# One transformer-like kernel: streamed expert weights, causal masks applied after the exponential, and logits and z taken at other places

## The chip, the cores and the metric

The kernel runs on one NeuronCore of a Trainium2 chip. TensorE multiplies matrices into PSUM, VectorE (DVE), ScalarE (ACT) and GpSimd (POOL) work on tiles, and SyncE (SP) issues most transfers. The metric is the device time of one launch in microseconds (us).

## What is computed

For each of 64 samples: an image of 224 x 224 x 3 becomes 196 patch tokens of width 192 (layer norm over a patch with its four shifted copies, then one product), 128 text tokens are appended, attention with 12 heads is added, and a soft mixture of 64 experts is added. T = 324 tokens, D = 192, hidden width F = 768.

```python
# attention, 12 heads of 16, with a sink column
att = jnp.einsum('bhqd,bhkd->bhqk', q, k) * scale
att = jnp.where(causal[None, None], att, -jnp.inf)
att = jnp.concatenate([sink_col, att], axis=-1)
att = jax.nn.softmax(att, axis=-1)[..., 1:]
y = jnp.einsum('bhqk,bhkd->bhqd', att, v)
# experts
logits = jnp.einsum('sd,btd->bst', sl, tok)
dispatch_w = jax.nn.softmax(logits, axis=-1)
combine_w = jax.nn.softmax(logits, axis=-2)
y = jnp.einsum('btd,bst->bsd', xn, dispatch_w)
y = jnp.einsum('sio,bsi->bso', fc1_weight, y) + fc1_bias
y = jax.nn.gelu(y, approximate=False)
y = jnp.einsum('sio,bsi->bso', fc2_weight, y) + fc2_bias
out = jnp.einsum('bsd,bst->btd', y, combine_w)
```

## The kernel before

There are four stages. A prologue folds the norms into the weights. Then a software pipeline runs over the samples: step `b` works on attention of sample `b`, the embedding of `b + 2`, the q/k/v preparation of `b + 1` and the expert routing of `b - 1`. Every engine has its program for a step written out by hand; the engines meet only through semaphores (`Signal`), and each engine runs its own list strictly in order. The third stage runs the 64 experts over the routed tokens of all samples, the fourth mixes the expert outputs back into the residuals and stores them.

One step on TensorE: a first loop over 12 heads computes `scores` (query by key, only to find each row's maximum, which DVE takes with `negmax`). Between heads stand parts of other work: `turn(z)` at head 3, the logits (slots by `zt`) at heads 7 and 8, the transposed maxima (`maxima`) at head 8, the transposed logits at head 10. A second loop over 12 heads computes `scores_t` (key by query, with the maximum already subtracted through extra rows of `qst`), ACT exponentiates into `prob`, and `values` multiplies `prob` by `vaug` in three groups of four heads. Each group has three products, k = 0, 1, 2, one for each key tile. `scores_t` of head h waits until the exponential of head h - 2 is done, because there are two pairs of PSUM banks. Groups 0 and 1 are multiplied inside the second loop, group 2 behind it, then come the projections (`project`), the head transposes, `proj` and the next step.

The mask: `causal` holds -1e30 above the diagonal; in both loops a small product with the identity adds it to the diagonal block of the scores. In `scores_t` that is three products a head (127, 128 and 69 columns).

DVE in a step: the maxima of the 12 heads, `lmax` and `dmax` of the routing softmax, `stat1`, `h_new` and its norm `mv1` for sample `b + 2`, `xhat`, the divided heads, the rotary products `by_cos` and `by_sin`, the residual `h1`, its norm `mv2`, and z. GpSimd: `rot`, `rest`, the chain from `alpha` to `beta_t` (the logits' scale), the split of the maxima (`mpart`), `part`, then `rstd1` and `rstd2` for sample `b + 2`. ACT: among others z squared, `zt`, the first maxima `mt`, the scaled logits `logit`, `dexp` (right ahead of the 12 exponentials), the exponentials, `comb` and `yraw`.

In the expert stage, a slot is one expert. SP keeps eight slots of weights in flight and refills two when a `down` product is done. For each slot TensorE multiplies with a 97 x 128 block of `w1` stationary and the 64 samples of `y_all` moving (12 products), ACT takes the gelu, and `down` multiplies `act_t` (stationary) by `w2` (moving, 192 columns). DVE adds biases that SP has loaded broadcast over the samples. In the last stage groups of four samples are loaded, multiplied (`cw` by `ow`), added by DVE and stored by ACT's queue.

## Time and profile before

| | us |
|---|---|
| median of 3 runs | 3379.23 (3373.21 to 3383.34) |
| the profiled execution | 3375.94 |
| its span, first to last instruction | 3374.2 |
| steps of samples, about 220 to 2850 | 40.96 each |
| experts | 2853 to 3220 |
| wait, then mixing and stores | 3220 to 3374 |

The profiled execution's own time is 1.7 us above its span. PE is TensorE's matmuls, PEld its weight loads, which overlap them; the end of a matmul is modelled, so the distance from one start to the next says more than a duration. An fp32 product stands as two records in the trace. A number in square brackets behind a row is idle time of that engine ahead of it, and what ended it.

### The profile page before, as it was taken

What the parts mean: (1) busy time and instruction counts of PE and PEld (TensorE: products, weight loads), DVE (VectorE), ACT (ScalarE), POOL (GpSimd) and SP (SyncE); (2) the same over time, 40 slices, a digit from 0 to 9 for tenths busy, and PEclk for the clock granted to TensorE, in tenths of its full rate; (3) what the DMA queues carried; (4) which work ended last, traced back from release to release, by engine and by line L of the source; (5) the groups of instructions that cost most, each with busy time, mean ns of one, the idle gap of its engine ahead of it and who ended that gap; (6) DMA issues with size and microseconds to landing.
All of it is one profiled execution on the core that took longest, in us unless ns stands there. A gap on an engine that the chain in (4) does not pass through costs nothing. (4 is left out here: it accounts for less than half of the span.)

```text
span 3374.2 us, 76729 instructions
## 1 busy us (share of the span) xinstructions
PE 2923.5 (87%) x27714; PEld 2267.1 (67%) x27714; DVE 1702.9 (50%) x5384; ACT 1625.0 (48%) x3266; POOL 1220.0 (36%) x2197
## 2 busy tenths in 40 slices
PE   3079999999999999999999999999999986999945
PEld 2057777777777777777777777777777765888832
DVE  2436666666656566556666666666565552000023
ACT  0045665566666666666666655666665653000000
POOL 2134444444444444444444444444444441000000
PEclk8589999999999999999999999999999997776778
DMA  4233333333333333333333333333333322988979
GB/s 107 48 79 86 90 91 92 87 93 88 88 88 88 89 87 88 86 86 86 86 86 90 92 92 91 88 88 87 88 89 88 86 58 57 231 226 227 233 199 292
DMA packets 445437, 364.24 MB, mean 108 GB/s; under 512 B 32526, under 2 KB 424091, under 8 KB 444828
## 3 DMA queue, kind: packets, MB, share of 16 engines
q1 hardware_dynamic: 420956, 342.23, 39.4%
q10 hardware_dynamic: 24128, 17.42, 1.6%
q8 instruction: 207, 3.39, 0.4%
q14 instruction: 146, 1.20, 0.1%
HBM read 199.61 MB, written 43.25 MB: 72 GB/s over the span
## 5 line engine op out<-in xcount | busy, mean ns | idle before, releaser
L959 DVE TENSOR_REDUCE negmax<-ps 128x1 f32<-128x325 f32 (+2 forms) x2304 | 665.1, 350 | 100.1 <-PE ps L605 92.3
L560 PE MATMUL ps<-window_w,xp 108*98 108x193 f32 x2304 | 507.4, 339 | 107.2 <-ACT xp L812 107.2
L812 ACT ACTIVATE prob<-ps 128x590 f32<-128x590 f32 x768 | 505.2, 662 | 185.1 <-PE ps L628 170.4
L603 PE MATMUL ps<-kst,qst 99*128 99x325 bf16 (+2 forms) x2304 | 394.5, 251 | 82.9 <-DVE negmax L959 82.9
L560 PEld LDWEIGHTS ps<-window_w,xp 108*98 108x98 f32 x2304 | 338.5, 167 | 110.6 <-ACT xp L812 107.3
L1147 POOL TENSOR_TENSOR rot<-by_cos,by_sin 96x324 f32<-96x324 f32 x128 | 111.8, 873 | 682.0 <-DVE by_sin L1043 681.9
L603 PEld LDWEIGHTS ps<-kst,qst 99*128 99x128 bf16 (+1 forms) x2304 | 224.0, 104 | 195.4 <-DVE negmax L959 116.5
L605 PE MATMUL ps<-causal,ident_b 128*128 128x128 bf16 (+1 forms) x2304 | 333.6, 213 | 0.0
L769 PE MATMUL ps<-xt,wqk 97*96 97x324 f32 (+1 forms) x1024 | 320.6, 446 | 1.7 <-ACT xt L812 1.7
L644 PE MATMUL ps<-prob,vaug 128*32 128x324 f32 (+2 forms) x4608 | 286.4, 341 | 0.1
L1277 PE MATMUL ps<-y_all,w 97*128 (+3 forms) x1536 | 233.8, 326 | 29.9 <-DMA w<-in_L_ffn_fc_weight_dram 29.0
L1277 PEld LDWEIGHTS ps<-y_all,w 97*128 97x128 f32 (+1 forms) x1536 | 227.1, 238 | 43.3 <-issue 34.2
L1030 DVE RECIPROCAL rden<-ps 98x12 f32<-98x12 f32 (+1 forms) x192 | 43.4, 226 | 381.3 <-PE ps L788 381.3
L622 PE MATMUL ps<-qst,kst 102*128 102x295 bf16 x768 | 228.6, 298 | 2.5 <-ACT prob L812 1.3
L812 ACT ACTIVATE xp<-xw 108x1764 f32<-108x1764 f32 x64 | 219.8, 3434 | 8.2 <-DMA xw<-in_x_dram 8.2
L605 PEld LDWEIGHTS ps<-causal,ident_b 128*128 128x128 bf16 (+1 forms) x2304 | 203.7, 103 | 14.7 <-issue 0.3
L769 PEld LDWEIGHTS ps<-xt,wqk 97*96 97x96 f32 (+1 forms) x1024 | 157.5, 165 | 83.2 <-issue 4.9
L1351 DVE TENSOR_TENSOR pair_out<-ps,biases 128x192 f32<-128x192 f32 x32 | 11.5, 358 | 359.1 <-PE ps L1264 311.5
L1318 ACT ACTIVATE act_t<-ps 128x384 f32<-128x384 f32 x64 | 31.4, 491 | 329.9 <-PE ps L1277 329.9
L625 PE MATMUL ps<-qst,kst 102*128 102x197 bf16 x768 | 189.8, 247 | 0.0
L1093 POOL TENSOR_TENSOR by_cos<-rot,part 96x648 f32<-96x648 f32 x128 | 185.4, 1468 | 0.0
L1127 POOL TENSOR_TENSOR part<-by_cos,part 96x648 bf16<-96x648 f32 x128 | 177.8, 1409 | 15.6 <-DMA qst<-part 12.9
(179 smaller groups left out, 6161.8 us busy)
## 6 DMA issues: line engine op xcount, KB each, us to landing
w<-in_L_ffn_fc_weight_dram SPq DMA_DIRECT2D x128, 576.0 KB
xw<-in_x_dram SPq DMA_DIRECT2D x384, 189.0 KB
qst<-part SPq DMA_DIRECT2D x768, 60.8 KB
kst<-part SPq DMA_DIRECT2D x768, 60.8 KB
h_held<-h_new SPq DMA_DIRECT2D x64, 288.0 KB, 4.3
residual_image<-h SPq DMA_DIRECT2D x64, 147.0 KB
h_i<-residual_image SPq DMA_DIRECT2D x16, 588.0 KB
out_dram<-h_i ACTq DMA_DIRECT2D x32, 294.0 KB
```

The costliest lines, as they stand in the source:

```text
L560: mm = pe.matmul(ps[0:TILE, BK7, half * (D + 1):(half + 1) * (D + 1)], xp[:, q, TILE * half:TILE * (half + 1)], window_w[:, q, :], start=( ...
L603: pe.matmul(ps[0:nq, bk, col:col + keys], qst[i][0:MAX_ROW, h, q0:q0 + nq], kst[i][0:MAX_ROW, h, 0:keys], start=True, stop=False)
L605: mm = pe.matmul(ps[0:nq, bk, col + q0 + 1:col + keys], ident_b[:, 0:nq], causal[:, 0:nq], start=False, stop=True)
L622: pe.matmul(ps[:, bank, 0:EXPC], k0, q[:, 0:EXPC], start=True, stop=False)
L625: pe.matmul(ps[:, bank + 1, c1:c2], k1, q[:, KTILES[1][2]:T], start=True, stop=False)
L644: mm = pe.matmul(ps[STRIP * s:STRIP * (s + 1), BK6, q0:T], vaug[i][0:nk, k, h, :], prob[0:nk, h % 8, col:col + T - q0], start=(k == 0), st ...
L769: mm = pe.matmul(ps[0:HALF, SC + 2 * side + e, 0:T], wqk[0:k, c, 2 * side + e, :], xt[0:k, c, 1:KEYS], start=(c == 0), stop=(c == 1))
L812: return nc.scalar.activation(out_, in_, f, **kw)
L959: last = dve.tensor_reduce(negmax[0:nq, q, h:h + 1], ps[0:nq, bk, col:col + q0 + nq + 1], AX.X, ALU.max, negate=True)
L1093: pool.tensor_tensor(rest[:, side], rot[:, side], part[0][:, side], ALU.subtract).then_inc(rest_ready.sem, 1)
L1127: pool.tensor_tensor(part[2][:, side], rest[:, side], part[1][:, side], ALU.subtract).then_inc(p3_ready.sem, 1)
L1277: mm = pe.matmul(ps[:, k % 4, B * f:B * (f + 1)], w1[k][0:kk, c, 128 * f:128 * (f + 1)], y_all[0:kk, c, one(s + k), :].rearrange("p o b -> ...
```

## The change

Attention. The three mask products of each head leave `scores_t`. Instead the diagonal blocks of the probabilities are set to zero after the exponential: for groups 0 and 1 by GpSimd (`affine_select`, three instructions a group, 4 x 127, 4 x 128 and 4 x 69 elements a partition), for group 2 by DVE (minimum with the tile `cap`, which is 1e30 or 0). `values` now waits for `capped` where it waited for the exponential. `prob` has 12 buffers in place of 8, groups 0 and 1 of `values` stand one head later, and the third product of group 1 behind the loop. ACT scales the logits ahead of the copy of the first maxima. DVE makes z behind the maxima of the next step's head 1, where it stood at the end of the step. The residuals and combine weights are stored in another layout, so that a group of four samples is one run for each partition.

Experts. Two slots go together. The samples of `y_all` are stationary and `w1` moves (384 columns at a time, the two slots in the two halves of the array's columns); the hidden layer is turned by six transposes (`turn`) and copied by DVE; the second bias is a product of its own. Weight rows are loaded as 6144 bytes of `w1` and 4608 bytes of `w2` for each partition in one run, where they were runs of 3072 and 768 bytes. All loops are written out.

```diff
-    himg = nc.dram_tensor("residual_image", (2 * B, TILE, D), F32, kind="Internal").ap()
-    htxt = nc.dram_tensor("residual_text", (B, TXT, D), F32, kind="Internal").ap()
-    cscr = nc.dram_tensor("combine_weights", (B, NS, T), F32, kind="Internal").ap()
+    himg = nc.dram_tensor("residual_image", (B // GROUP, TILE, GROUP, 2, D), F32, kind="Internal").ap()
+    htxt = nc.dram_tensor("residual_text", (B // GROUP, TXT, GROUP, D), F32, kind="Internal").ap()
+    cscr = nc.dram_tensor("combine_weights", (B // GROUP, 2, NS, GROUP // 2, T), F32, kind="Internal").ap()
...
+                        dve.wait_ge(cap_mm, 1)
+                        dve.tensor_scalar(cap[:], ps[:, 5, 0:128], -1.0, 1.0, ALU.max, ALU.add)
+                        dve.drain()
+                        dve.tensor_scalar(cap[:], cap[:], -MASKED, None, ALU.mult)
...
+                def cap_probs(engine, b, g):
+
+                    exp_ready.wait(engine, b, 4 * g + 4)
+                    h0, col = 4 * g, 0
+                    for k, (_, nk, q0) in enumerate(KTILES):
+                        first = 1 if k == 0 else 0
+                        nq = min(128, T - q0) - first
+                        p = prob[0:nk, h0:h0 + 4, col:col + nq]
+                        if g < 2:
+                            last = engine.affine_select(p, p, [[0, 4], [1, nq]], ALU.is_ge, 0.0, base=first,
+                                                        channel_multiplier=-1)
+                        else:
+                            allowed = cap[0:nk, first:first + nq].unsqueeze(1).broadcast_to((nk, 4, nq))
+                            last = engine.tensor_tensor(p, p, allowed, ALU.min)
+                        col += T - q0
+                    last.then_inc(capped.sem, 1)
...
-                        pe.matmul(ps[:, bank, 0:EXPC], k0, q[:, 0:EXPC], start=True, stop=False)
-                        pe.matmul(ps[:, bank, 0:127], causal[:], ident_b[:, 1:128], start=False, stop=True)
+                        pe.matmul(ps[:, bank, 0:EXPC], k0, q[:, 0:EXPC], start=True, stop=True)
                         pe.matmul(ps[:, bank + 1, 0:n0], k0, q[:, EXPC:T], start=True, stop=True)
-                        pe.matmul(ps[:, bank + 1, c1:c2], k1, q[:, KTILES[1][2]:T], start=True, stop=False)
-                        pe.matmul(ps[:, bank + 1, c1:c1 + 128], causal[:], ident_b[:], start=False, stop=True)
-                        pe.matmul(ps[:, bank + 1, c2:EXPC], k2, q[:, KTILES[2][2]:T], start=True, stop=False)
-                        pe.matmul(ps[:, bank + 1, c2:EXPC], causal[:], ident_b[:, 0:EXPC - c2], start=False,
-                                  stop=True).then_inc(st_mm.sem, 1)
+                        pe.matmul(ps[:, bank + 1, c1:c2], k1, q[:, KTILES[1][2]:T], start=True, stop=True)
+                        pe.matmul(ps[:, bank + 1, c2:EXPC], k2, q[:, KTILES[2][2]:T], start=True, stop=True
+                                  ).then_inc(st_mm.sem, 1)
...
-                            exp_ready.wait(pe, b, 4 * g + 4)
+                            capped.wait(pe, b, g + 1)
...
-                            if att and h in (5, 6, 7, 9, 10, 11):
-                                values(b, i, h // 4 - 1, (h - 1) % 4)
+                            if att and h in (6, 7, 8, 10, 11):
+                                values(b, i, h // 10, (h - 6) % 4)
...
+                        if att:
+                            values(b, i, 1, 2)
...
+                        if moe:
+
+                            l_mm.wait(act, b - 1)
+                            beta_ready.wait(act, b - 1)
+                            for t, (_, nt) in enumerate(TTILES):
+                                last = fn(logit[0:nt, t, :], ps[0:nt, BK5, NS * t:NS * (t + 1)], ACT.Copy,
+                                          scale=beta_t[0:nt, t:t + 1])
+                            last.then_inc(l_scaled.sem, 1)
...
-                                if h >= 8:
-                                    pv_mm.wait(act, b, 1)
-                                elif h % 4 == 0:
-                                    pv_mm.wait(act, b - 1)
-                                fn(prob[:, h % 8, :].rearrange("p (a q) -> p a q", a=2),
+                                if h % 4 == 0:
+                                    pv_mm.wait(act, b - 1, h // 4 + 1)
+                                fn(prob[:, h, :].rearrange("p (a q) -> p a q", a=2),
...
-                            if att and h in (7, 11):
-                                heads_out(b, h // 4 - 1)
+                            if att and h in (9, 11):
+                                heads_out(b, h // 11)
...
+                            if moe and h == 1:
+
+                                ln2_ready.wait(dve, b - 1)
+                                ym_mm.wait(dve, b - 2)
+                                zs_ready.wait(dve, b - 2)
+                                for t, (_, nt) in enumerate(TTILES):
+                                    last = dve.scalar_tensor_tensor(out=z[0:nt, t], in0=h1[0:nt, t], scalar=mv2[0:nt, t, 0:1],
+                                                                    in1=nwb[0:nt], op0=ALU.subtract, op1=ALU.mult)
+                                last.then_inc(z_ready.sem, 1)
...
                         if att:
+                            capped.wait(dve, b, 2)
+                            cap_probs(dve, b, 2)
...
                         if att:
                             maxima_parts(b, 1)
+                            cap_probs(pool, b, 0)
...
+                        if att:
+                            cap_probs(pool, b, 1)
+                        if front:
```

```diff
+            PAIRS, NPAIR, FH = 4, NS // 2, F // 2
+            w1, w2 = tiles("w1_", [HALF + 1, 2, F], 2 * PAIRS), tiles("w2_", [128, FC, D], 2 * PAIRS)
+            hidden, act_t = tiles("hidden", [2 * B, F], 2), tiles("act_t", [128, FC, 2 * B], 2)
+            pair_out = tiles("pair_out", [2 * B, D], PAIRS)
+            b2_all = tiles("b2_all", [NS, D], 1)[0]
...
-                def load_slot(s, k):
-                    sp.dma_start(w1[k][0:HALF], fc1[one(s)].rearrange("o (c p) f -> p (o c) f", c=2)).then_inc(w_in[k], 16)
-                    sp.dma_start(w1[k][HALF:HALF + 1, 0, :], b1[one(s)]).then_inc(w_in[k], 16)
-                    sp.dma_start(w2[k][:], fc2[one(s)].rearrange("o (c p) d -> p (o c) d", c=FC)).then_inc(w_in[k], 16)
+                def load_up(n):
+                    p = n % PAIRS
                     for j in range(2):
+                        s = 2 * n + j
+                        sp.dma_start(w1[2 * p + j][0:HALF], fc1[s].rearrange("(p c) f -> p c f", c=2)).then_inc(w1_in[p], 16)
+                        sp.dma_start(w1[2 * p + j][HALF:HALF + 1, 0, :].rearrange("o (a f) -> o a f", a=16),
+                                     b1[s:s + 1].rearrange("o (a f) -> o a f", a=16)).then_inc(w1_in[p], 16)
+
+                def load_down(n):
+                    p = n % PAIRS
                     for j in range(2):
+                        sp.dma_start(w2[2 * p + j][:], fc2[2 * n + j].rearrange("(p c) d -> p c d", c=FC)).then_inc(w2_in[p], 16)
+
...
+                for n in range(PAIRS):
+                    load_up(n)
+                    load_down(n)
+                    if n == 0:
+                        sp.dma_start(b2_all[:], b2).then_inc(b2_in, 16)
+                for n in range(PAIRS, NPAIR):
+                    sp.wait_ge(up_mm, n - PAIRS + 1)
+                    load_up(n)
+                    sp.wait_ge(down_mm, n - PAIRS + 1)
+                    load_down(n)
+                    store_pair(n - PAIRS)
...
-                        for f in range(FC):
-                            for c in range(2):
-                                kk = HALF + 1 - c
-                                mm = pe.matmul(ps[:, k % 4, B * f:B * (f + 1)], w1[k][0:kk, c, 128 * f:128 * (f + 1)],
-                                               y_all[0:kk, c, one(s + k), :].rearrange("p o b -> p (o b)"),
-                                               start=(c == 0), stop=(c == 1))
-                        mm.then_inc(up_mm, 1)
...
+                def up(n):
+                    p, bank = n % PAIRS, 2 * (n % 2)
+                    pe.wait_ge(w1_in[p], 64 * (n // PAIRS + 1))
+                    if n >= 2:
+                        pe.wait_ge(gelu_ready, n - 1)
+                    for h in range(2):
+                        for c in range(2):
+                            kk = HALF + 1 - c
+                            for j in range(2):
+                                mm = pe.matmul(ps[B * j:B * (j + 1), bank + h, 0:FH], y_all[0:kk, c, 2 * n + j, :],
...
+                def turn(n):
+                    pe.wait_ge(gelu_ready, n + 1)
+                    if n >= 1:
+                        pe.wait_ge(turned, n)
+                    for c in range(FC):
+                        mm = pe.transpose(ps[:, 4 + c // 3, 128 * (c % 3):128 * (c % 3 + 1)], hidden[n % 2][:, c:F:FC], ident[:])
+                    mm.then_inc(turn_mm, 1)
...
+                def down(n):
+                    p = n % PAIRS
+                    pe.wait_ge(turned, n + 1)
+                    pe.wait_ge(w2_in[p], 32 * (n // PAIRS + 1))
+                    if n == 0:
+                        pe.wait_ge(b2_in, 16)
+                    if n >= 2:
+                        pe.wait_ge(pair_ready, n - 1)
+                    for j in range(2):
+                        s = 2 * n + j
+                        pe.matmul(ps[B * j:B * (j + 1), 6 + n % 2, 0:D], ident[0:NS, s:s + 1].broadcast_to((NS, B)), b2_all[:],
+                                  start=True, stop=False, skip_group_check=True)
+                    for c in range(FC):
                         for j in range(2):
+                            mm = pe.matmul(ps[B * j:B * (j + 1), 6 + n % 2, 0:D], act_t[n % 2][:, c, B * j:B * (j + 1)],
+                                           w2[2 * p + j][:, c, :], start=False, stop=(c == FC - 1), skip_group_check=True)
                     mm.then_inc(down_mm, 1)
 
+                for m in range(NPAIR + 2):
+                    if m < NPAIR:
+                        up(m)
+                    if 0 <= m - 1 < NPAIR:
+                        turn(m - 1)
+                    if 0 <= m - 2:
+                        down(m - 2)
```

GpSimd's list from the end of the second maxima split, before:

```order
L1083 TENSOR_TENSOR mpart1<-mrest,mpart1 128x3x6
L1134 TENSOR_TENSOR rstd1<-stat1 98x2 [waits stat_ready]
L1136 TENSOR_TENSOR rstd1<-stat1,rstd1 98x2
L1138 TENSOR_SCALAR rstd1<-rstd1 98x2
L1070 TENSOR_TENSOR rstd1<-rstd1,neg_half 98x2
L1142 TENSOR_TENSOR rstd2<-mv1,eps 128x3 [waits ln1_ready]
L1070 TENSOR_TENSOR rstd2<-rstd2,neg_half 128x3
L1147 TENSOR_TENSOR rot<-by_cos,by_sin 96x324 [waits rope_ready]
```

and in the change:

```order
L1113 TENSOR_TENSOR mpart1<-mrest,mpart1 128x3x6
L496 AFFINE_SELECT prob<-prob 128x4x127 [waits exp_ready]
L496 AFFINE_SELECT prob<-prob 128x4x128
L496 AFFINE_SELECT prob<-prob 69x4x69
L1165 TENSOR_TENSOR rstd1<-stat1 98x2 [waits stat_ready]
L1167 TENSOR_TENSOR rstd1<-stat1,rstd1 98x2
L1169 TENSOR_SCALAR rstd1<-rstd1 98x2
L1100 TENSOR_TENSOR rstd1<-rstd1,neg_half 98x2
L1174 TENSOR_TENSOR rstd2<-mv1,eps 128x3 [waits ln1_ready]
L1100 TENSOR_TENSOR rstd2<-rstd2,neg_half 128x3
L496 AFFINE_SELECT prob<-prob 128x4x127 [waits exp_ready]
L496 AFFINE_SELECT prob<-prob 128x4x128
L496 AFFINE_SELECT prob<-prob 69x4x69
L1182 TENSOR_TENSOR rot<-by_cos,by_sin 96x324 [waits rope_ready]
```

Three selects stand ahead of `rstd1` and three between `rstd2` and `rot`; the first waits for the exponentials of heads 0 to 3 (`exp_ready`), the fourth for those of heads 4 to 7.

TensorE around the first product of `values`, from `scores_t` of head 5, before (`prob` by `vaug` is `values`):

```order
L622 MATMUL ps<-qst0,kst0 128x295 [waits exp_ready]
L623 MATMUL ps<-ident_b,causal 128x127
L624 MATMUL ps<-qst0,kst0 128x29
L625 MATMUL ps<-qst0,kst0 128x197
L626 MATMUL ps<-ident_b,causal 128x128
L627 MATMUL ps<-qst0,kst0 128x69
L628 MATMUL ps<-ident_b,causal 128x69
L644 MATMUL ps<-prob,vaug0 32x324 [waits de_ready,v_ready,exp_ready]
L644 MATMUL ps<-prob,vaug0 32x324 x3
L622 MATMUL ps<-qst0,kst0 128x295 [waits exp_ready,max_in1]
```

and in the change, from the same head:

```order
L650 MATMUL ps<-qst0,kst0 128x295 [waits exp_ready]
L651 MATMUL ps<-qst0,kst0 128x29
L652 MATMUL ps<-qst0,kst0 128x197
L653 MATMUL ps<-qst0,kst0 128x69
L650 MATMUL ps<-qst0,kst0 128x295 [waits exp_ready,max_in1]
L651 MATMUL ps<-qst0,kst0 128x29
L652 MATMUL ps<-qst0,kst0 128x197
L653 MATMUL ps<-qst0,kst0 128x69
L669 MATMUL ps<-prob,vaug0 32x324 [waits de_ready,v_ready,capped]
L669 MATMUL ps<-prob,vaug0 32x324 x3
L763 MATMUL ps<-ident,lexp 64x98 [waits c_ready,zt_ready,prepared]
```

The three masks of a head are gone, `values` stands behind head 6, and its first product waits for `capped`.

DVE at the turn from one step to the next, before (`bn2` and `mv2` are the norm of `h1`):

```order
L945 BN_AGGR mv2<-bn2 98x2 x2
L945 BN_AGGR mv2<-bn2 128x2
L1060 SCALAR_TENSOR_TENSOR z<-h1,mv2,nwb 98x192 [waits zs_ready,ym_mm]
L1060 SCALAR_TENSOR_TENSOR z<-h1,mv2,nwb 98x192
L1060 SCALAR_TENSOR_TENSOR z<-h1,mv2,nwb 128x192
L959 TENSOR_REDUCE negmax<-ps 128x1 [waits s_mm,mpart_ready]
L959 TENSOR_REDUCE negmax<-ps 68x1
L959 TENSOR_REDUCE negmax<-ps 128x1
L959 TENSOR_REDUCE negmax<-ps 128x1 [waits s_mm]
L959 TENSOR_REDUCE negmax<-ps 68x1
```

and in the change:

```order
L970 BN_AGGR mv2<-bn2 98x2 x2
L970 BN_AGGR mv2<-bn2 128x2
L984 TENSOR_REDUCE negmax<-ps 128x1 [waits s_mm,mpart_ready]
L984 TENSOR_REDUCE negmax<-ps 68x1
L984 TENSOR_REDUCE negmax<-ps 128x1
L984 TENSOR_REDUCE negmax<-ps 128x1 [waits s_mm]
L984 TENSOR_REDUCE negmax<-ps 68x1
L984 TENSOR_REDUCE negmax<-ps 128x1
L993 SCALAR_TENSOR_TENSOR z<-h1,mv2,nwb 98x192 [waits zs_ready,ym_mm,ln2_ready]
L993 SCALAR_TENSOR_TENSOR z<-h1,mv2,nwb 98x192
L993 SCALAR_TENSOR_TENSOR z<-h1,mv2,nwb 128x192
L984 TENSOR_REDUCE negmax<-ps 128x1 [waits s_mm]
```

The maxima of heads 0 and 1 now come ahead of z.

## Rows read from the trace of the kernel before

**Rows 1.** Stretches: span, busy of each engine, PEclk, DMA share, GB/s.
```profile
1541.00:1582.00 41.00, 38.36 (x395) 29.53 (x394) 24.93 (x83) 24.93 (x51) 18.61 (x34) 1.00 0.33 87
...
2853.00:3220.00 367.00, 337.76 (x2304) 301.44 (x2304) 11.10 (x31) 32.71 (x65) 2.77 (x4) 0.72 0.92 229
3220.00:3248.00 28.00, 0.32 (x5) 0.06 (x1) 0.36 (x1) 0.00 (x0) 0.00 (x0) 0.58 0.56 126
3248.00:3374.00 126.00, 78.04 (x192) 37.73 (x192) 47.59 (x96) 0.00 (x0) 0.00 (x0) 0.84 0.92 276
```

**Rows 2.** Timeline of PE: start, duration, instruction; `scores_t` of head 0.
```profile
1500.72 0.29 PE L622 MATMUL ps<-qst,kst 102*128 102x295 bf16 x1
1500.85 0.22 PE L623 MATMUL ps<-ident_b,causal 128*128 128x127 bf16 x1
1500.91 0.18 PE L624 MATMUL ps<-qst,kst 102*128 102x29 bf16 x1
...
1501.12 0.20 PE L628 MATMUL ps<-ident_b,causal 128*128 128x69 bf16 x1
1501.15 0.54 PE L560 MATMUL ps<-window_w,xp 108*98 108x193 f32 x2
```

**Rows 3.** Timeline of PE: its waits in one step.
```profile
1529.58 0.31 PE L603 MATMUL ps<-kst,qst 99*128 99x325 bf16 x1 [1.22 <-DVE negmax L959]
...
1539.65 0.44 PE L717 MATMUL ps<-ident,logit 98*64 98x98 f32 x3 [1.30 <-ACT logit L812]
...
1541.68 0.29 PE L622 MATMUL ps<-qst,kst 102*128 102x295 bf16 x1
```

**Rows 4.** Timeline of PE: first product of `values`, groups 1 and 2.
```profile
1510.05 0.75 PE L644 MATMUL ps<-prob,vaug 128*32 128x324 f32 x8
...
1514.25 1.21 PE L644 MATMUL ps<-prob,vaug 128*32 128x324 f32 x24
```

**Rows 5.** Timelines of DVE: z in a step and in the last one.
```profile
1526.25 2.46 DVE L1060 SCALAR_TENSOR_TENSOR z<-h,mv,nwb 98x192 f32<-98x192 f32 x3 [0.16 <-issue]
...
2837.97 1.08 DVE L1060 SCALAR_TENSOR_TENSOR z<-h,mv,nwb 98x192 f32<-98x192 f32 x3 [0.16 <-issue]
```

**Rows 6.** Timelines of POOL, ACT and DVE between the two loops.
```profile
1536.24 0.22 POOL L1083 TENSOR_TENSOR mpart<-mrest,mpart 128x18 bf16<-128x18 f32 x1
...
1537.46 0.43 ACT L812 ACTIVATE mt<-ps 18x324 bf16<-18x324 bf16 x1 [1.02 <-PE ps L672]
...
1541.48 0.48 DVE L971 TENSOR_REDUCE dmax<-ps 64x1 f32<-64x324 f32 x1
...
1542.52 2.07 ACT L812 ACTIVATE prob<-ps 128x590 f32<-128x590 f32 x3
```

**Rows 7.** Timeline of POOL: from `stat1` to `rstd2`.
```profile
1505.94 0.20 POOL L1134 TENSOR_TENSOR rstd<-stat 98x2 f32<-98x2 f32 x1 [3.97 <-DVE stat L998]
...
1510.34 0.87 POOL L1070 TENSOR_TENSOR rstd<-rstd,neg_half 128x3 f32<-128x3 f32 x1
```

**Rows 8.** A memset on POOL (timeline); two groups of instructions: busy us, mean ns.
```profile
2853.05 2.77 POOL L1340 MEMSET ow<- 128x768 f32 x4 [8.46 <-POOLq L305]
...
L1093 POOL TENSOR_TENSOR by_cos<-rot,part 96x648 f32<-96x648 f32 x24 | 34.9, 1473 | 0.0
...
L1043 DVE TENSOR_TENSOR by_cos<-ps,cos_t 96x648 f32<-96x648 f32 x24 | 19.8, 824 | 5.8 <-PE ps L769 5.8
```

**Rows 9.** Timeline of PE: one `down`, then the up products of two slots.
```profile
2902.47 2.17 PE L1264 MATMUL ps<-w,act_t 128*64 128x192 f32 x24
2904.57 5.57 PE L1277 MATMUL ps<-y_all,w 97*128 x48
```

**Rows 10.** DMA issues: KB, median us to landing; PE timeline of other fp32 products.
```profile
centred_weights<-wn SPq DMA_DIRECT2D x1, 2880.0 KB, 8.3
...
1515.39 2.43 PE L769 MATMUL ps<-xt,wqk 97*96 97x324 f32 x8
1517.66 1.15 PE L788 MATMUL ps<-ident,yraw 128*98 128x128 f32 x9
```

258 lines of the change are left out of this document (108 added, 150 removed).

## The prediction

> **What bounds the kernel now.** I first read the stretches [rows 1]. A step of attention has TensorE busy for 38.36 of 41.00 us at granted clock 1.00; DVE and ACT have 24.93 each, GpSimd 18.61. So a step is TensorE's list, plus the few places where it waits. Two starts of the same product, 1500.72 and 1541.68 [rows 2, 3], give the step: 40.96 us. Next came the timeline of TensorE with its waits [rows 3]: 1.22 us at head 2 of the first loop for the maximum of head 0, and 1.30 us for the scaled logits. Nothing else in a step is over 0.2 us. The experts' 367 us are another matter: TensorE busy 338 us at clock 0.72, the DMA engines 92% busy at 229 GB/s. Both are near full there. Behind it stand 28 us of waiting and 126 us of mixing at 92% DMA share and 276 GB/s [rows 1].
>
> **What attention gains on TensorE.** The masks: from the start of a mask product to the next start are 0.06, 0.06 (the second is like the first) and 0.03 us [rows 2], so 0.15 a head and 1.8 us a step. The wait of 1.22 us goes, since the maxima of heads 0 and 1 are taken before z. z then also runs later than the large GpSimd products; it takes 1.08 us in the last step, where none is beside it, and 2.46 in a full one [rows 5], so DVE gets up to 1.4 us back. The wait of 1.30 us shrinks: the split maxima are there at 1536.46 (1536.24 + 0.22), their transposes and the ACT copy of 0.43 us follow [rows 6], and with some 0.3 us for the transposes and 0.1 a hand-over the logits' transposes start near 1537.6, not 1539.65 [rows 3]: 2.0 us earlier for both waits together. If that were all, a step would be 3.8 us shorter.
>
> **What takes its place.** I follow the chain that `capped` makes, in the times of this step.
> 1. DVE has head 9's maxima, `lmax`, and the maxima of heads 10 and 11 to do in a row before `dmax`. By my count `dmax` starts 1.2 us earlier than 1541.48, not 2.0, and with it the first exponential, at 1541.3 in place of 1542.52 [rows 6].
> 2. Three exponentials take 2.07 us [rows 6]. `scores_t` of head 2 needs the first one done (1542.0), and has 0.9 us of TensorE work between its start and that of head 3, so exponential 3 ends near 1544.2. GpSimd's first three selects run from 1544.3 to 1544.3 + c, where c is what a group costs.
> 3. Only then comes `rstd1`. From its start to the end of `rstd2` are 5.27 us (1505.94 to 1510.34 + 0.87) [rows 7], DVE's `h_new` and norm in it. The second group of selects ends at 1549.6 + 2c.
> 4. `values` of group 1 starts 0.1 us later. Before it started at 1510.05 + 40.96 = 1551.01 [rows 2 to 4]. The change here is 2c - 1.3 us.
> 5. From there to group 2 were 4.2 us (1510.05 to 1514.25) [rows 4]. Now: a product (0.7), `scores_t` of head 11 (0.3), its exponential (0.7), hand-overs (0.2), then DVE's minimum over 1296 elements a partition. DVE's `by_cos` takes 824 ns for 648 [rows 8], so 1.65 us. That is 3.6 us, 0.6 less than before.
>
> So a step changes by 2c - 1.9 us. All that stands behind group 2 is unchanged. Queued behind TensorE's wait for `capped` are head 11 and everything up to the next step; ACT and DVE wait with it. Where the first group waits (TensorE is at head 6 near 1545.3) costs nothing of its own as long as the second group is later.
>
> **The price c.** No select is in this trace. A group is 1296 elements a partition in three instructions. From below: GpSimd's memset of 768 elements takes 0.69 us (2.77 for four), 0.90 ns an element, so 1.17 us. From above: its two-input products take 1473 ns for 648, 2.27 ns an element [rows 8], so 2.95 us. A select reads one tensor in place of none or two; I take 1.6 us, nearer the memset, with a little for the read and the comparison. Then a step is 1.3 us longer, and over the 61 steps that hold all four parts +79 us. At the ends of the range: +0.4 a step (+27 us) and +4.0 (+244 us).
>
> On this the Trainium skill ("GPSIMD Engine Reference", section 3.1) has a number: about 1.8 cycles an element at best for a tight loop at 1.2 GHz. As an estimate that makes 1.9 us a group, and by it the step would be 2.0 us longer, +122 us. It lies inside the two rows.
>
> **Experts.** The stretch moves 367 us x 229 GB/s = 84 MB [rows 1]. The broadcast biases fall away (64 x 48 KB, 3 MB), which leaves 81 MB, 2.53 MB for each of 32 pairs: 11.0 us at 229 GB/s. The fastest large transfer here is 2880 KB in 8.3 us, 355 GB/s, with runs of 23 KB [rows 10]; at that rate a pair takes 7.1 us. TensorE at full clock: four fp32 products of 324 columns take 2.27 us (1515.39 to 1517.66) [rows 10], 1.75 ns a column. The two slots of a pair run side by side: `down` has 12 products of 192 columns in 2.17 us [rows 9], where one after the other would be 4.0. So up is 4 x 384 columns, 2.7 us; `down` with its bias 7 rounds of 0.36, 2.5 us; the turn six transposes at 1.15 us for nine [rows 10], 0.8 us. Together 6.0 us a pair, against 5.57 + 2.17 = 7.7 now [rows 9]. At the present clock of 0.72 it would be 8.3. I take 7.6 us a pair, between transfers at 355 GB/s and TensorE at 0.72: 243 us and 9 for the first load, 252 in place of 367, -115. ACT's gelu and DVE's copies are under 2 us a pair and hide. The 28 us behind it are mostly four group loads ahead of the last stores: -8. The mixing loads come in longer runs, its 768-byte stores stay: -13 of 126. In all -136, with ends of -100 and -168.
>
> **Sum.** The profiled execution is 3375.9 us (span 3374.2), 3.3 below the median. 3375.9 + 79 - 136 = 3319 us. The prologue's one transpose and two small DVE operations, and TensorE's strided reads of z, I cost at nothing: z's load is unchanged in length, and the prologue's work lies beside transfers.
>
> **The rivals.**
> - *Forecast*: select between 1.17 and 1.9 us a group, experts well faster. Own range 3235 to 3370. Chance 0.47.
> - *Attention gains too.* If a group of selects costs under 0.95 us, or exponentials or `rstd1` come earlier than I count by 1 to 2 us, TensorE keeps part of its 3.8 us. At one us a step gained: 3375.9 - 61 - 136 = 3179. For it: ACT and GpSimd have slack on average. Against: the memset row alone gives 1.17. Chance 0.15.
> - *The second group of selects decides, and the kernel is slower.* Place: `values` of group 1 behind `rstd2`. At the two-input price a step is 4.0 us longer: 3375.9 + 244 - 100 = 3520. The total turns slower by over 0.3% when 61 x (2c - 1.9) is over 146, at c = 2.15. For it: all GpSimd rows with arithmetic are dear. Chance 0.22.
> - *Longer runs bring nothing.* The experts stay at 229 GB/s, 11.0 us a pair: -4 there, some -20 in all, 3375.9 + 79 - 20 = 3435. For it: the DMA share of 92% says nothing about which run is slow. Against: 355 GB/s was moved here. Chance 0.09. The Trainium skill ("DMA: Bandwidth & Descriptors", Specifications) speaks for it: it puts the smallest transfer at line rate at 512 bytes, and the runs of 768 are above that.
> - Several of these at once, or something else: 0.07.
>
> Some 0.3% (10 us) is what a measurement can tell from no change. From the cases: faster 0.65 (the forecast nearly whole, the second, a little of the third), within 0.3% 0.07, slower 0.28. The range 3190 to 3460 leaves out the better part of "gains too" and the dear end of the third.
>
> **What would show it.** In the changed profile: selects of 0.4 to 0.7 us each; TensorE's largest wait in a step at the first product of group 1 for GpSimd; no wait at head 2 of the first loop; a step of 42.3 us; DVE's minimum ahead of group 2 at 1.65 us; the experts at 300 to 330 GB/s and 250 to 260 us. It is wrong if a select is over 0.9 us or under 0.3, if `rstd1` isn't what the second group of selects waits behind, or if the experts' stretch stays over 330 us, be it by the transfers or by a clock that falls further.

## The result: 7% slower

The changed kernel takes 3621.1 us (median of four runs, 3616.7 to 3624.5) where the kernel before takes 3381.3 (median of four) in the same comparison. The ratio is 1.071, with a 95% interval of 1.068 to 1.074. The forecast was 3319 us, in a range up to 3460; both its sign and its range missed. The profiled execution has a span of 3622.8 us against 3374.2, 248.6 more.

First the page of the changed kernel: the granted clock of TensorE in 40 equal slices, in tenths (9 is 90% or more), and three groups of its fifth part:

```profile
PEclk8589999999999998999989999999999998578888
...
L669 PE MATMUL ps<-prob,vaug 128*32 128x324 f32 (+2 forms) x4608 | 377.2, 448 | 211.8 <-POOL prob L496 208.0
...
L496 POOL TENSOR_SCALAR_AFFINE_SELECT prob<-prob 128x508 f32<-128x508 f32 (+2 forms) x384 | 233.5, 652 | 169.0 <-ACT prob L839 169.0
L500 DVE TENSOR_TENSOR prob<-prob,cap 128x508 f32<-128x508 f32 (+2 forms) x192 | 105.0, 603 | 155.8 <-ACT prob L839 155.8
```

The value products now wait 208 us in all for the selects. A group of selects (three of 384) costs 233.5 / 128 = 1.82 us, a group of minima 105.0 / 64 = 1.64 us.

The stretches, with the columns of [rows 1]: two of attention, the experts, the gap behind them, the mixing.

```profile
300.00:1300.00 1000.00, 872.54 (x7758) 641.86 (x7761) 570.86 (x1840) 536.47 (x1094) 485.46 (x880) 0.91 0.30 79
1300.00:2300.00 1000.00, 875.89 (x7855) 644.68 (x7848) 574.49 (x1851) 543.70 (x1102) 485.37 (x880) 0.91 0.30 79
3155.00:3479.00 324.00, 249.08 (x1600) 134.93 (x1600) 41.75 (x63) 27.02 (x33) 2.56 (x4) 0.82 0.96 255
3479.00:3497.00 18.00, 0.15 (x2) 0.00 (x0) 0.36 (x1) 0.00 (x0) 0.00 (x0) 0.63 0.47 122
3497.00:3622.00 125.00, 81.16 (x192) 39.50 (x192) 47.55 (x96) 0.00 (x0) 0.00 (x0) 0.83 0.90 278
```

Beside [rows 1]: the experts begin at 3154.8 us, where they began at 2853.1; they take 324 us for 367, the gap 18 for 28, the mixing as long as before. So 302 us were lost in attention and 53 won behind it. In attention TensorE is busy a smaller part of the time (0.87 for 0.94) and has lost its full clock: 0.91 where it was 1.00.

How much longer is a step? The transposes of the maxima come six times a step, in 64 steps. Here are their instructions' durations with the first and the last start, for before and for after:

```profile
L672 PE MATMUL ps<-ident_b,mpart x384: 192/217/314, 226.4 to 2815.7; 128*18 128x128 bf16 x128, 68*18 68x68 bf16 x64
```
```profile
L697 PE MATMUL ps<-ident_b,mpart x384: 191/217/314, 227.2 to 3109.4; 128*18 128x128 bf16 x128, 68*18 68x68 bf16 x64
```

From the first to the last are 2589.3 and 2882.2 us, over 63 steps 4.65 us a step more: 45.6 for the 40.96 of the step in [rows 2, 3]. The steps below are read in the same way. Per step TensorE idles 5.8 us (0.1275 x 45.6; before 2.64) and is busy 39.8 (before 38.36, of which 1.8 have gone with the masks).

One step of after (43.6 us long, one of the short ones) shows the place. The timeline of GpSimd:

```profile
1518.98 1.83 POOL L496 TENSOR_SCALAR_AFFINE_SELECT prob<-prob 128x508 f32<-128x508 f32 x3 [2.20 <-ACT prob L839]
1520.79 0.19 POOL L1165 TENSOR_TENSOR rstd<-stat 98x2 f32<-98x2 f32 x1
...
1521.86 0.72 POOL L1100 TENSOR_TENSOR rstd<-rstd,neg_half 98x2 f32<-98x2 f32 x1
1524.85 0.19 POOL L1174 TENSOR_TENSOR rstd<-mv,eps 128x3 f32<-128x3 f32 x1 [2.27 <-DVE mv L970]
1525.18 0.87 POOL L1100 TENSOR_TENSOR rstd<-rstd,neg_half 128x3 f32<-128x3 f32 x1
1526.00 1.84 POOL L496 TENSOR_SCALAR_AFFINE_SELECT prob<-prob 128x508 f32<-128x508 f32 x3
```

And of TensorE:

```profile
1520.70 0.30 PE L650 MATMUL ps<-qst,kst 102*128 102x295 bf16 x1 [0.89 <-DMA qst<-mt]
1521.08 0.75 PE L669 MATMUL ps<-prob,vaug 128*32 128x324 f32 x8
...
1524.14 0.29 PE L650 MATMUL ps<-qst,kst 102*128 102x295 bf16 x1
...
1527.89 1.27 PE L669 MATMUL ps<-prob,vaug 128*32 128x324 f32 x8 [3.32 <-POOL prob L496]
1529.09 0.43 PE L650 MATMUL ps<-qst,kst 102*128 102x295 bf16 x1
...
1532.80 1.21 PE L669 MATMUL ps<-prob,vaug 128*32 128x324 f32 x24
```

GpSimd follows the chain of the prediction to the tenth of a microsecond: selects, `rstd1`, an idle 2.27 us for VectorE's norm, `rstd2`, selects. TensorE waits 3.32 us for the second selects, which the formula of the prediction holds. What the prediction did not have comes after the wait: the same eight value products that took 0.75 us at 1521.08 take 1.27 at 1527.89, and `scores_t` 0.43 for 0.29. The windows of 4 us around it, columns as above, show why:

```profile
1524.00:1528.00 4.00, 0.68 (x12) 0.47 (x14) 2.87 (x10) 1.60 (x4) 2.85 (x5) 1.00 0.36 95
1528.00:1532.00 4.00, 4.00 (x39) 2.21 (x38) 1.42 (x3) 1.10 (x2) 0.00 (x0) 0.57 0.00 0
1532.00:1536.00 4.00, 4.00 (x42) 2.61 (x41) 0.22 (x1) 3.08 (x5) 0.00 (x0) 1.00 0.02 4
```

TensorE idled, then worked at a granted clock of 0.57 over the next 4 us, mostly at the lower of its two levels (1.2 GHz for 2.4), and then had the full clock again. This step has the shortest such stretch. In the next one the wait is 3.53 us, and two windows behind it are low:

```profile
1572.00:1576.00 4.00, 4.00 (x38) 3.13 (x35) 1.64 (x3) 1.17 (x3) 0.00 (x0) 0.55 0.09 22
1576.00:1580.00 4.00, 4.00 (x34) 2.21 (x33) 0.00 (x0) 1.91 (x5) 0.00 (x0) 0.60 0.00 0
```

No step of the changed kernel keeps the full clock: the means of single steps lie at 0.96, 0.92 or 0.89 nearly throughout, and the lower the clock, the longer the step (about 43.6, 45.2 and 47 us). Before, with waits of 1.22 and 1.30 us [rows 3], it held 1.00. The Trainium skill ("TensorE: Matmul & The Clock Gate", Part 1) says that the throttled clock is the default state and that activity releases it; the rows agree as far as they go.

### The profile page after: what moved, and what is told of

Same layout as the page of the kernel before. It is cut to its first block and busy times, and to the rows that moved or that the text cites. A ratio compares the mean times of both kernels' runs of the same rounds, so it can differ in the third digit from the quotient of the medians.

```text
span 3622.8 us, 70062 instructions
## 1 busy us (share of the span) xinstructions
PE 2951.8 (81%) x24707; PEld 2100.2 (58%) x24707; DVE 1813.6 (50%) x5610; ACT 1606.3 (44%) x3234; POOL 1442.9 (40%) x2581
## 5 line engine op out<-in xcount | busy, mean ns | idle before, releaser
L669 PE MATMUL ps<-prob,vaug 128*32 128x324 f32 (+2 forms) x4608 | 377.2, 448 | 211.8 <-POOL prob L496 208.0
L669 PEld LDWEIGHTS ps<-prob,vaug 128*32 128x32 f32 (+1 forms) x4608 | 139.7, 137 | 349.4 <-POOL prob L496 222.2
L796 PE MATMUL ps<-xt,wqk 97*96 97x324 f32 (+1 forms) x1024 | 340.6, 468 | 1.7 <-ACT xt L839 1.7
L496 POOL TENSOR_SCALAR_AFFINE_SELECT prob<-prob 128x508 f32<-128x508 f32 (+2 forms) x384 | 233.5, 652 | 169.0 <-ACT prob L839 169.0
L631 PEld LDWEIGHTS ps<-kst,qst 99*128 99x128 bf16 (+1 forms) x2304 | 225.8, 104 | 119.9 <-DVE negmax L984 39.8
L796 PEld LDWEIGHTS ps<-xt,wqk 97*96 97x96 f32 (+1 forms) x1024 | 168.6, 177 | 96.1 <-issue 28.6
L650 PEld LDWEIGHTS ps<-qst,kst 102*128 102x128 bf16 x768 | 78.6, 102 | 193.3 <-issue 71.8
L1285 PE MATMUL ps<-w,y_all 97*64 97x384 f32 (+1 forms) x512 | 127.7, 658 | 75.8 <-DMA w<-in_L_ffn_fc_bias_dram 75.8
L500 DVE TENSOR_TENSOR prob<-prob,cap 128x508 f32<-128x508 f32 (+2 forms) x192 | 105.0, 603 | 155.8 <-ACT prob L839 155.8
```

What stands on the lines that cost most here:

```text
L496: last = engine.affine_select(p, p, [[0, 4], [1, nq]], ALU.is_ge, 0.0, base=first, channel_multiplier=-1)
L631: pe.matmul(ps[0:nq, bk, col:col + keys], qst[i][0:MAX_ROW, h, q0:q0 + nq], kst[i][0:MAX_ROW, h, 0:keys], start=True, stop=False)
L650: pe.matmul(ps[:, bank, 0:EXPC], k0, q[:, 0:EXPC], start=True, stop=True)
L669: mm = pe.matmul(ps[STRIP * s:STRIP * (s + 1), BK6, q0:T], vaug[i][0:nk, k, h, :], prob[0:nk, h, col:col + T - q0], start=(k == 0), stop=( ...
L796: mm = pe.matmul(ps[0:HALF, SC + 2 * side + e, 0:T], wqk[0:k, c, 2 * side + e, :], xt[0:k, c, 1:KEYS], start=(c == 0), stop=(c == 1))
L1285: mm = pe.matmul(ps[B * j:B * (j + 1), bank + h, 0:FH], y_all[0:kk, c, 2 * n + j, :], w1[2 * p + j][0:kk, c, FH * h:FH * (h + 1)], start=( ...
```

## The experiments

Each ratio below is against runs of the kernel before taken beside that kernel (medians 3374.7 to 3378.5 us); differences between two changed kernels are differences of medians from such separate comparisons, so a few us of them are noise.

**Are attention and experts two separate matters?** `e1_old_experts` is the changed attention with the old experts, mixing, scratch layouts and halves of z:

```diff
-    himg = nc.dram_tensor("residual_image", (B // GROUP, TILE, GROUP, 2, D), F32, kind="Internal").ap()
+    himg = nc.dram_tensor("residual_image", (2 * B, TILE, D), F32, kind="Internal").ap()
...
-                                                   z[0:nt, t, c:D:2], disp[0:nt, t, :],
+                                                   z[0:nt, t, HALF * c:HALF * (c + 1)], disp[0:nt, t, :],
```

> The changed attention stage with the expert and mixing stages, scratch layouts and unstrided z columns of before. If the loss sits wholly in the attention stage (first key maxima to expert start: 45.6 us a step against 40.95, 63 steps, +284 us) and the experts and the gap behind them brought 42 + 10 us, this kernel takes 3621 + 52 = 3673 us (3655 to 3690). Rival: the new scratch layouts or the strided z columns are part of what slows the attention stage; then its steps are shorter than 45.6 us and the time is below 3640 us.

It took 3677.8 us, ratio 1.089 (1.087 to 1.091). `e10_only_experts` is its mirror image: the kernel before with the new experts and layouts only.

> The kernel before with only the changed experts, scratch layouts and strided z columns; its attention stage, masks on TensorE and orders stay. e1 showed 52 to 57 us between the old and the new experts behind the changed attention stage. If the two halves of the change are independent: step 41.0 us, clock 1.00, 3378 - 55 = 3323 us (3310 to 3335). Rival (the new layouts cost the attention stage's stores something): above 3340 us.

It took 3330.7 us, 0.988 (0.985 to 0.990). The granted clock in attention is 0.91 in e1 and 1.00 in e10, as with the attention stage each has. So the halves are independent within some 13 us: the new experts, mixing and layouts bring 57 us behind the changed attention and 44 behind the old one, and the whole loss is attention's.

**Is it the selects or the new order?** `e2_masks_back` puts the three small mask products a head back into `scores_t` and drops the selects and minima; all of the new order stays:

```diff
-                        pe.matmul(ps[:, bank, 0:EXPC], k0, q[:, 0:EXPC], start=True, stop=True)
+                        pe.matmul(ps[:, bank, 0:EXPC], k0, q[:, 0:EXPC], start=True, stop=False)
+                        pe.matmul(ps[:, bank, 0:127], causal[:], ident_b[:, 1:128], start=False, stop=True)
...
-                            capped.wait(pe, b, g + 1)
+                            exp_ready.wait(pe, b, 4 * g + 4)
```

> The changed kernel with the masks of the transposed scores back on TensorE (three small products a head, 1.8 us a step) and no selects and minima; logits ahead, z behind, twelve probability buffers, value order and new experts stay. Theory A (the wait for GpSimd's second group of selects costs twice: 3.4 us of idle TensorE a step and, behind it, a stretch at half the granted clock worth 3.5 us): granted clock 0.99 or more in the stage, step 39 to 40.5 us, 3230 to 3330 us in all, likeliest 3270. Theory B (the longer step comes from the order of the work: z behind, the value products one head on, the late second maxima): clock stays near 0.91, step 44 us or more, 3540 us or more.

It took 3306.5 us, ratio 0.979 (0.977 to 0.982), with the clock back at 1.00 and 0.99 in the two stretches. Theory B falls. But against e10, which has the old order, the new order is worth only 24 us, and the step is on average only 0.16 us shorter than before (2579.4 us from first to last transposes, for 2589.3). The waits of TensorE from 300 to 2800 us (61 steps) tell where the expected gain went (us in total, times, longest):

```profile
PE ps L700 <- POOL mpart L1113: 49.9, 61, 2.4
PE ps L672 <- ACT yraw L842: 45.3, 61, 0.7
PE ps L650 <- DMA qst<-mt: 24.1, 61, 1.7
PE ps L631 <- DVE negmax L987: 21.2, 68, 1.8
```

Together they are 2.3 us a step, where the two waits of 1.22 and 1.30 us stood. The last is the rest of the wait for the maxima; the prediction had none of the other three.

**Is it where the second selects stand?** `e3_select_first` moves one call on GpSimd's list, ahead of the wait for the norm's statistics:

```diff
+                        if att:
+                            cap_probs(pool, b, 1)
                         if front:
                             ln1_ready.wait(pool, b + 2)
                             pool.tensor_tensor(rstd2[:], mv1[:, :, 1], eps[:], ALU.add)
                             power(rstd2[:], rstd2[:], neg_half[:]).then_inc(rstd2_ready.sem, 1)
-                        if att:
-                            cap_probs(pool, b, 1)
```

> Only the place of GpSimd's selects of heads 4 to 7 moves: ahead of the wait for the statistics of rstd2 instead of behind rstd2. Exponential 7 ends near 1523.3 us in the shown step, the selects began at 1526.0. Theory A: the selects start 2.7 us earlier, TensorE's wait at value group 1 falls from 3.4 us to under 1 us, the granted clock returns to 0.98 or more, the step is 39.4 to 41 us, and the time 3240 to 3340 us. With the idle time alone and the clock staying at 0.91 (the clock falls for another reason): step 42.9 us, 3450 us. Theory B (GpSimd is simply too full, the wait moves on to rstd2 and xhat): step 45 us or more, 3580 us or more.

It took 3267.5 us, 0.967 (0.964 to 0.969): 354 us less than the changed kernel, by one call. Its timelines, GpSimd, TensorE and VectorE:

```profile
1521.00 0.74 DVE L1039 SCALAR_TENSOR_TENSOR h_new<-ps,rstd,hb 98x192 f32<-98x192 f32 x2 [2.79 <-POOL rstd L1100]
...
1521.49 1.65 POOL L496 TENSOR_SCALAR_AFFINE_SELECT prob<-prob 128x508 f32<-128x508 f32 x3 [0.53 <-ACT prob L839]
1523.57 0.87 POOL L1100 TENSOR_TENSOR rstd<-rstd,neg_half 128x3 f32<-128x3 f32 x1
...
1523.64 0.75 PE L669 MATMUL ps<-prob,vaug 128*32 128x324 f32 x8 [0.90 <-ACT yraw L839]
1524.48 0.96 DVE L1056 TENSOR_SCALAR xhat<-h_new,mv,rstd 98x192 f32<-98x192 f32 x3 [1.02 <-POOL rstd L1100]
...
1527.27 1.21 PE L669 MATMUL ps<-prob,vaug 128*32 128x324 f32 x24
```

The selects run in the time in which GpSimd had idled. `rstd2`'s power starts 2.57 us behind `h_new`, as in the changed kernel (1522.61 to 1525.18), so it isn't delayed, and the value products wait 0.90 us for another thing, ScalarE's copy `yraw`. From them to group 2 (1527.27) are 3.6 us, the very number of the prediction's step 5; in the changed kernel they were 4.9, at the lower clock. The stage runs at 0.99 to 1.00 and a step is 1.0 us shorter than before (2526.4 us from first to last transposes, for 2589.3).

**Is it the idling that costs the clock?** e3 takes idling and clock away together. `e4_filler` takes the idling away by work without use, just ahead of the waiting product, and touches nothing else:

```diff
+                            if att and h == 10:
+                                for n in range(FILL):
+                                    pe.matmul(ps[:, BK5, 256:512], kst[i][0:STACK, 10, 0:128],
+                                              kst[i][0:STACK, 10, 0:256], start=True, stop=True)
```

> The changed kernel with 28 products without use (128 x 256 columns in bf16, into unread columns of a bank, about 0.11 us each, 3.0 us in all) put on TensorE just where it waits 3.4 us for the selects of heads 4 to 7. Nothing else changes; the filler's results are read by nobody. Theory A (the idle wait is what brings the clock down): granted clock 0.98 or more, wait at value group 1 under 0.8 us, step 42 us, 3380 to 3450 us, although TensorE does more. Rival (the clock falls for another reason, or the lower clock costs nothing because the chain through GpSimd sets the step): clock stays near 0.91 or the step stays at 45.6 us, 3610 us or more.

It took 3415.5 us, ratio 1.011 (1.008 to 1.014). TensorE does 3.2 us more a step, and the kernel is 206 us faster than the changed one. The timeline of TensorE, and a stretch of attention:

```profile
1513.51 3.22 PE L760 MATMUL ps<-kst 102*128 102x256 bf16 x28
1516.97 0.75 PE L670 MATMUL ps<-prob,vaug 128*32 128x324 f32 x8 [0.24 <-POOL prob L497]
```
```profile
300.00:1300.00 1000.00, 932.78 (x9038) 710.61 (x9036) 615.00 (x1990) 578.83 (x1184) 522.89 (x953) 1.00 0.33 86
```

The group's products take 0.75 us again, and the clock is 1.00. The step is 1.5 us longer than before (2685.9 us from first to last transposes), and the experts' loads start at 2959.5 us, 106.4 later than before. So of attention's 301.7 us, 106.4 are the chain through the selects, and 195.3 go with the clock that falls when TensorE idles on it (these are the profiled executions; the medians of all runs give 206). The rival, another reason for the clock, falls.

These kernels can be laid beside the forecast part by part. These are medians over 57 steps of each trace, in us, from the start of the first exponential to the first value product of group 1, from there to group 2, and from there to the next first exponential (the forecast's values follow from its steps 1 to 5 with c = 1.6):

| | forecast | before | changed | e4 | e3 | e2 |
|---|---|---|---|---|---|---|
| first exponential to group 1 | 11.6 | 8.50 | 11.83 | 11.81 | 9.30 | 10.09 |
| group 1 to group 2 | 3.6 | 4.20 | 5.93 | 3.63 | 3.63 | 3.58 |
| group 2 to next exponential | 27.1 | 28.25 | 28.01 | 26.86 | 26.89 | 26.89 |
| step | 42.3 | 40.96 | 45.37 | 42.30 | 39.87 | 40.59 |

With the clock kept (e4) every part comes out as forecast, within 0.3 us. That the sum agrees to the tenth is luck, since c, which counts twice, was 0.2 too low. The changed kernel has the same 11.8 us up to group 1. It loses 2.3 us between groups 1 and 2 and 1.2 behind group 2.

**What bounds the new experts?** The next four kernels are built on e3. `e5_fewer_products` leaves out half of the up products and five of six chunks of the down products:

```diff
-                        for c in range(2):
...
-                    for c in range(FC):
+                    for c in range(1):
```

> e3 (the changed kernel with the selects of heads 4 to 7 ahead of rstd2), and in the expert stage half of the up products and five of six chunks of the down products left out; all loads, stores, transposes and copies stay. The output is then not the reference's. In e3 the stage lasted 341 us with the DMA engines busy 0.99 of it. If the transfers set the stage: 320 to 340 us, the wait of the up products for their weights grows by what the products shrink. If TensorE at its lower clock set it: 250 to 280 us.

One execution took 3252.5 us. Its experts' stretch, and TensorE's wait there:

```profile
2797.00:3106.00 309.00, 187.01 (x704) 79.58 (x704) 41.96 (x64) 26.89 (x33) 2.42 (x4) 0.53 1.01 267
```
```profile
PE ps L1283 <- DMA w<-in_L_ffn_fc_bias_dram: 122.8, 32, 8.0
```

With less than half of TensorE's instructions it still lasts 309 us, with the DMA engines' share at 1.01. That is 11 us under what I expected of a stage set by its transfers, and far from 250 to 280.

`e6_w1_short` and `e7_w2_short` each give one of the two weights its old, shorter runs back (3072 bytes for 6144, 768 for 4608), with the columns of z or of the hidden layer in the order that goes with it:

```diff
-fc1[s].rearrange("(p c) f -> p c f", c=2)
+fc1[s].rearrange("(c p) f -> p c f", c=2)
...
-fc2[2 * n + j].rearrange("(p c) d -> p c d", c=FC)
+fc2[2 * n + j].rearrange("(c p) d -> p c d", c=FC)
```

> e3 with the first expert weights loaded in pieces of 3072 B as before (rows p and 96 + p on a partition, z columns in halves) instead of 6144 B. Packets of 6144 B took 404 to 425 ns on average, pieces of 3072 B in the kernel before 194 ns. If the time of a packet goes by its bytes: stage 331 to 341 us, total within 10 us of e3, rather less than more. If longer runs helped: the stage is 15 us or more longer.

> e3 with the second expert weights loaded in pieces of 768 B as before instead of 4608 B. Six pieces of 768 B took 6 x 49 = 294 ns in the kernel before, one of 4608 B 244 to 271 ns: 8192 x 23 to 50 ns over 16 engines, 12 to 26 us more: 3279 to 3293 us. If the length of the runs is what bounds the stage: 50 us or more. If only bytes count: nothing, within 5 us of e3.

They took 3272.3 us, 0.969 (0.966 to 0.971), and 3277.0 us, 0.972 (0.968 to 0.975): neither can be told from e3 (0.967, 0.964 to 0.969). The length of the runs is worth nothing here that I can measure. e7 lies 10 us over e3, where 12 to 26 were expected; a loss of that size isn't excluded. No run has both weights in short pieces. Runs of one kernel scatter by 41 us in e7; in the profiled executions the experts' stretch took 340 us in e3, 329 in e6 and 308 in e7. A single profile of this stretch tells no 20 us apart, and so e5's 309 us can't be told from e7's 308 with all its products.

`e8_two_queues` moves the loads of the second weights to ScalarE's queue, where they are issued behind its gelu and the wait for `down`:

```diff
-                        sp.dma_start(w2[2 * p + j][:], fc2[2 * n + j].rearrange("(p c) d -> p c d", c=FC)).then_inc(w2_in[p], 16)
+                        act.dma_start(w2[2 * p + j][:], fc2[2 * n + j].rearrange("(p c) d -> p c d", c=FC)).then_inc(w2_in[p], 16)
```

> e3 with the loads of the second expert weights issued on ScalarE's queue instead of SyncE's, so that two queues feed the 16 engines. If the engines are simply full (0.99 busy): no change, within 10 us of e3. If one queue with its order of first weights, bias row, second weights holds transfers back: 15 to 60 us faster, 3207 to 3252 us.

It took 3250.0 us, 0.962 (0.961 to 0.964), 17 us under e3 by the medians and 14 by the ratios: at the near edge of the range expected if one queue holds transfers back. The intervals of e3 and e8 just touch, so a gain is likely; its size and cause are open. The Trainium skill ("DMA: Bandwidth & Descriptors", Rules for kernel authors) says that spreading transfers over issuing engines brings no bandwidth; these runs neither confirm that nor clearly refute it.

**A better version.** `e9_copy_earlier` is e8 with ScalarE's copy of value group 0 one exponential earlier, `e11_maxima_earlier` is e9 with the second maxima's transposes one head earlier:

```diff
-                            if att and h in (9, 11):
+                            if att and h in (8, 11):
                                 heads_out(b, h // 11)
...
-                            if att and h == 2:
+                            if att and h == 1:
                                 l_scaled.wait(pe, b - 1, apart=True)
```

> e8 (selects of heads 4 to 7 ahead of rstd1 and rstd2's wait, two load queues) with ScalarE's copy of value group 0 behind exponential 8 instead of 9. In e3 the value products of group 1 waited 0.9 us a step for that copy. If that wait is on the path: 0.4 to 0.9 us a step, 25 to 55 us, 3195 to 3225 us. Rival: the copy delays exponential 9 and with it the same products by its own 0.5 us, within 15 us of e8's 3250 us.

> e9 with the transposes of the second maxima behind transposed scores of head 1 instead of head 2, so that their copy and store start about 0.7 us earlier. In e3 TensorE waited 0.6 to 0.8 us a step at head 6 for that store. If the store is what is late: 0.3 to 0.7 us a step, 20 to 45 us under e9. Rival: GpSimd's parts of the maxima are not ready then (they ended 0.8 us ahead of the old place), TensorE waits there instead: within 10 us of e9.

e9 took 3223.9 us, 0.953 (0.950 to 0.956), 26 under e8, at the lower edge of what was expected: the wait for the copy has gone (52 us in e8 from 300 to 2600 us), and most of it came back as waits of the value products for selects and minima (43 us). (In e8 and e9 the selects stand behind `rstd1`, as in e3.) e11 took 3202.3 us, 0.948 (0.946 to 0.950), 22 under e9, but not for the reason I gave. The waits of TensorE in e11, 300 to 2600 us:

```profile
PE ps L697 <- POOL mpart L1113: 46.2, 62, 1.2
PE ps L650 <- DMA qst<-mt: 39.9, 54, 1.6
PE ps L669 <- POOL prob L496: 25.7, 57, 0.5
...
PE ps L650 <- ACT prob L839: 3.7, 5, 0.9
```

The wait for the store is what it was (37.4 us in e9); the one for the exponential fell from 24.0 us to 3.7. The transposes now stand, as I read it, where TensorE had waited for ScalarE; no run tests that.

**How long does TensorE itself need for the experts?** `e12_half_loads` is e11 with the first weights loaded for the first four pairs only:

```diff
-                    sp.wait_ge(up_mm, n - PAIRS + 1)
-                    load_up(n)
```

> e11 with the first expert weights and their bias rows loaded only for the first four pairs; the other 28 pairs reuse them, all products stay. The output is then not the reference's. It halves the bytes of the expert stage and leaves TensorE's work whole. My forecast had TensorE's work at 7.6 us a pair, 243 us, in its two-clock mix. If the transfers set the stage (about 285 us in e11) it falls to what TensorE needs: between 6.5 us a pair at 2.4 GHz (208 us) and 9.4 at 1.2 GHz (300 us), likeliest 215 to 245 us, total 3130 to 3165 us, and the up products wait for no weights. If the order of TensorE, ScalarE and VectorE within a pair set it: 280 us or more, total 3190 to 3205 us.

One execution took 3121.9 us. Its experts' stretch, and that of e11:

```profile
2752.00:2978.00 226.00, 205.19 (x1600) 125.38 (x1600) 41.94 (x64) 27.24 (x33) 2.77 (x4) 0.93 0.70 216
```
```profile
2758.00:3062.00 304.00, 235.97 (x1600) 132.14 (x1600) 42.11 (x64) 27.20 (x33) 2.53 (x4) 0.85 1.01 272
```

The same products with 49 MB in place of 83 (226 x 216 and 304 x 272): 226 us instead of 304, within the 215 to 245 expected of the stage; the whole kernel came out 8 us under its range. After the first pairs no up product waits for weights. So a pair takes 7.1 us where the weights don't hold it up, at a mean clock of 0.93, and 9.5 where they do. With e5 this shows from both sides that the transfers set the stage.

## Why the prediction was wrong

| stretch | forecast, us | measured | with TensorE kept busy (e4) |
|---|---|---|---|
| attention | +79 | +302 | +106 |
| experts | -115 | -43 | |
| gap | -8 | -10 | |
| mixing | -13 | 0 | |
| sum | -57 | +249 | |

**The chain through `capped` was right.** TensorE's largest wait is at the first product of group 1, behind `rstd2`. From the first exponential (1516.07) to the end of the second selects (1527.84) are 11.8 us; steps 1 to 3 give 11.9 with c = 1.82. The minima take 1.64 us (forecast 1.65), and no wait of 1.2 us is left at head 2. With c = 1.82 the formula 2c - 1.9 gives 1.7 us a step, 106 over 61 steps. e4 measured 1.3 us in the median step and 1.5 on average. That its stage also came out 106 us longer is in part luck: a few of its steps are 1.5 to 5 us longer than the rest.

**The price c was a little low**: 1.82 for 1.6, worth 27 us. The Trainium skill's number ("GPSIMD Engine Reference", section 3.1), 1.9 by the estimate made from it, was nearer than my choice between the rows.

**The step that failed is the sum behind the wait: "That is 3.6 us, 0.6 less than before" (step 5) and "So a step changes by 2c - 1.9 us. All that stands behind group 2 is unchanged."** The 3.6 us became 5.9 in the changed kernel, and what stands behind group 2 took 28.0 us where it takes 26.9 at the full clock. I took TensorE's durations from a trace in which it hardly waits and held its clock, and put a wait of over 3 us into it. All that stands behind that wait runs for a while at the lower level. That is worth 195 us, the greatest term of all, and the sum had no place for it. [rows 1] had held both clocks side by side: 1.00 in attention, 0.72 in the experts, where TensorE waits for loads. The sum used 0.72 to price the experts and never asked what would happen to 1.00. The prediction's last paragraph names a clock that falls, but for the experts alone. The rival that comes out slower had the place right and the point from which it decides wrong: c = 2.15 leaves the clock out.

**The experts' term was a third of its size.** "At that rate a pair takes 7.1 us" came from the one transfer of [rows 10], 355 GB/s; the stage moved 255 GB/s, 267 with TensorE at half its work and 272 with two queues. That one transfer was a store, from the tile `wn` to DRAM, by itself; the weights are loads. Whether the direction, the pieces of 23 KB or the company makes the difference, no run tests. My 7.6 us a pair was close to the 7.1 of e12, where the weights hold nothing up, and 10.1 is what came. The stage lies within the bound I gave for being wrong (330 us) and above the 250 to 260 us I expected. What was won, 43 us, is hardly the longer runs' doing, since e6 and e7 lost nothing measurable without them. My reading, which no run tests, is that the stage was TensorE's and the transfers' in about equal parts (338 of 367 us busy, DMA share 0.92 [rows 1]), and that the new products take TensorE out of it. *Longer runs bring nothing*, with a chance of 0.09, was right about the transfers and wrong in putting the gain at nothing. That these runs move 244 to 272 GB/s where another transfer had 355 stays unexplained.

**TensorE's gain in attention was mis-sized too.** The masks are worth their 1.8 us: busy time per step falls from 38.4 to 36.6 us in e3 (0.916 x 39.96). The earlier logits and z were to bring the first exponential 1.2 us forward, and it came 1.4 us forward: that much less lies between group 2 and it in e2, e3 and e4. From group 1 to group 2 are 0.6 us less as well. But in e2, which has neither selects nor minima, 1.6 us were lost again ahead of group 1 (10.1 us for 8.5), where the value products stand a head later and wait for `yraw`. So its median step is 0.4 us shorter, and the average 0.16.

**The mixing** gained nothing by longer loads: 126 us as before, where 13 less were forecast.

## What to carry to other kernels

When an edit puts a wait of several microseconds into TensorE's list where its granted clock is 1.00, price the clock behind the wait as well as the wait. Here the second cost nearly twice what the chain itself did (195 us and 106). Before work goes to an idle engine, find the place in that engine's list: the same selects make a step 5.6 us longer behind `rstd2` than ahead of it, in a hole that the trace shows as idle time of GpSimd. Work without use at the waiting place is a cheap test of whether the clock is at stake.
